# A fused gated cross-attention block: one transpose of a batch's maxima in place of two, and the maxima added to the queries in two parts

## The chip, the cores and the metric

The kernel runs on one core of a Trainium2 chip. The metric is the device time of one execution in microseconds (us); before the change the median of three runs is 1119.73 us (1119.67 to 1120.63).

## The reference, cut to what matters

The input is 128 batches of 128 tokens with 256 features, and a context of the same shape. Per batch (all fp32, 16 heads of D = 16 features):

```python
v = (ctx @ Wv + bv);  k = (ctx @ Wk + bk);  q = (layernorm(x) @ Wq + bq)     # 16 heads of 16
energy = einsum('nqhd,nkhd->nhqk', q, k);  energy = where(mask == 0, neg, energy)
attn = softmax(energy / sqrt(16), axis=-1)
x = x + tanh(g_xattn) * (einsum('nhqk,nkhd->nqhd', attn, v) @ Wo + bo)
x = x + tanh(g_ffn) * tanh(layernorm(x) @ W1 @ W2 @ W3 + b_ffn)
```

The softmax needs, for each head and query, the maximum over the keys. The change concerns how that maximum gets to the queries.

## The kernel before, in words

The 128 batches are worked in 64 pairs. Each engine has its own instruction list, written out by hand as a loop over t = 0..63, and semaphores between them; nothing is reordered at run time. A step of the loop has two halves, one batch each: half 0 handles batch 2t, half 1 batch 2t+1. The pair's projections, the output product and the feed-forward product of earlier pairs are put between the attention's pieces.

**The layout of a head.** The 128 partitions are four groups j of 32 rows. Each group holds one head in 16 of its rows; the four slots s = 2m + a (m, a = 0, 1) along the free axis hold the other heads, so 4 x 4 = 16 heads. `spread` (L720) writes q_aug and k_aug, 128 x 512 for each batch. It scales by `parity`, a 128 x 2 table with a one where the row is in half a of its group, so that slot s has its head's features in half a of each group of 32 rows and the other 16 rows are free. In k_aug one of the free rows is all ones (set through the bias, `one_row`, L858). In q_aug the same row later takes minus the query's maximum, so that one product of 32 rows gives score minus maximum.

**The chain of one batch i**, with the names of the code:

1. `scores(i)` (TensorE, L546): 32 matmuls give the scores, queries on partitions, in ps_s, four banks of PSUM; 16 small bf16 matmuls (L552) add the mask. It waits for `t_masked` of batch i-2, since ps_s is one buffer that two kinds of scores share.
2. `maxima(i)` (VectorE, L938): one reduction 128 x 2048 to 128 x 16 writes minus the maxima into neg_max, a tile of 144 columns: slot s of group j goes to column 16 + 32j + s.
3. `turn_max(i)` (TensorE, L563): two fp32 transposes by the identity, of columns 0 to 127 and of columns 16 to 143, into ps_x. The first puts the maxima of slot s into row 32j + 16 + s, the second into row 32j + s; all other rows are zero.
4. `append_max(i)` (VectorE, L944): one `tensor_tensor` 128 x 512 adds both results to q_aug, the first to the slots with a = 0, the second to those with a = 1, and signals `q_ready2`.
5. `scores_T(i)` (TensorE, L573): 32 matmuls give score minus maximum, keys on partitions, in ps_s again. It waits for `q_ready2` of batch i and for `max_ready` of batch i+1, since `maxima(i+1)` must have read ps_s.
6. `mask_transposed(i)` (VectorE, L949) adds the mask while it moves 128 x 2048 from ps_s to probs; ScalarE takes the exponents (L748); `weigh_values(i)` (TensorE, L585) multiplies by the values into ps_x and waits for `q_ready2` of batch i+2 too, since ps_x held its turned maxima.

In TensorE's list one half runs: `turn_max(i-1)`, `scores(i)`, `weigh_values(i-3)`, the output product (half 0, L455) or the turning of y and three quarters of v (half 1, L442 and L510), `scores_T(i-1)`, then the projections of q and k (half 0, L448) or the rest of v, the feed-forward product and the turning of x (half 1, L510, L455, L442).

In VectorE's list half 1 of a step, with the `append_max` that opens it, runs: `append_max`, moments of y (L964, L968), moments of x (L931), `maxima(2t+1)`, reciprocals (L974), statistics of x (L925), `low_of_y` (L905), `mask_transposed`. Half 0 runs: `append_max`, `low_of_x` (L905), statistics of x (L925), `maxima(2t)`, a transpose of the context (L910), the residual (L957), `mask_transposed`.

Of the kernel before, what the change touches and what calls it, by code (L numbers as in the profile page):

```python
# [10 lines left out]
ALU = mybir.AluOpType  # L11
AX = mybir.AxisListType

P = 128
E = 256
KT = E // P
H = 16
D = E // H
G = 4
ROWS = 2 * D  # L20
SLOTS = H // G
PAIR = 2
TOK = PAIR * P
# [7 lines left out]
def gated_xattn_block(nc, x, ctx, mask, g_xattn, g_ffn, Wv, bv, Wk, bk, Wq, bq, Wo, bo,  # L31
# [7 lines left out]
    out_v = out.rearrange("(p b) s e -> s p b e", b=PAIR)  # L39

    with ExitStack() as stack:
        def sb(name, shape, dt=F32):
            return stack.enter_context(nc.sbuf_tensor(name, shape, dt))

        def psum(name, shape):
            return stack.enter_context(nc.psum_tensor(name, shape, F32))

        def sem(name):
            return stack.enter_context(nc.semaphore(name))


        ident = sb("ident", [P, P])
# [5 lines left out]
        wq_raw, wk_raw, wv_raw, wo_raw = (sb(n, [P, KT, E]) for n in ("wq_raw", "wk_raw", "wv_raw", "wo_raw"))  # L58
# [3 lines left out]
        parity, one_row = sb("parity", [P, 2]), sb("one_row", [P, KT, 2])  # L62
# [16 lines left out]
        q_aug = [sb(f"q_aug{i}", [P, PAIR, SLOTS, P]) for i in range(2)]  # L79
        k_aug = [sb(f"k_aug{i}", [P, PAIR, SLOTS, P]) for i in range(2)]  # L80
        v_ones = [sb(f"v_ones{i}", [P, PAIR, H, 2 * D]) for i in range(V_RING)]
        neg_max = [sb(f"neg_max{i}", [P, D + P]) for i in range(2)]
        probs = [sb(f"probs{i}", [P, G, SLOTS, P]) for i in range(2)]
        a_den = [sb(f"a_den{i}", [P, 2, KT, PAIR, P]) for i in range(2)]
        a_rows, den_wide, a_norm = (sb(n, [P, KT * TOK]) for n in ("a_rows", "den_wide", "a_norm"))
# [15 lines left out]
        ps_s = psum("ps_s", [P, G, SLOTS, P])  # L101
        ps_x = psum("ps_x", [P, SLOTS, P])
# [20 lines left out]
        ffn_landed, out_landed, bf_landed = sem("ffn_landed"), sem("out_landed"), sem("bf_landed")  # L123
# [30 lines left out]
        def wait(eng, semaphore, value):  # L154
            if value > 0:
                eng.wait_ge(semaphore, value)
# [18 lines left out]
            return a.rearrange("p a b -> p (a b)")  # L175

        def heads_of(slot):
            return [(j, (slot // 2) * 2 * G + 2 * j + slot % 2) for j in range(G)]


        @block.sync
        def _(sp):
            def load_weight(dst, src, landed):
                sp.dma_start(dst[:], src.rearrange("(k p) n -> p k n", p=P)).then_inc(landed, 16)
# [4 lines left out]
            def load_x(p):  # L189
                wait(sp, y_ready, p - X_RING + 1)  # L190
                sp.dma_start(x_in[p % X_RING][:], x_v[:, p]).then_inc(x_landed[p % X_RING], 16)

            def load_ctx(p):
                wait(sp, ctx_turned, p - 1)
                if p == 0:
                    sp.dma_start(ctx_in[0][:], ctx_v[:, 0]).then_inc(ctx_landed[0], 16)
                    return
                for a in range(G):
                    rows = slice(a * 32, (a + 1) * 32)
                    sp.dma_start(ctx_in[p % 2][rows].rearrange("c n (b e) -> c (n b) e", e=64),  # L200
                                 ctx[PAIR * p:PAIR * (p + 1), :, a * 64:(a + 1) * 64].rearrange("n (b c) e -> c (n b) e", c=32)
                                 ).then_inc(ctx_landed[p % 2], 16)
# [18 lines left out]
            def wo_rows(src, m):  # L221

                return src.rearrange("(m j a d) n -> m a j d n", m=KT, a=2, d=D)[m]

            def load_later():
                for dst, src in ((w2_s, W2), (w3_s, W3), (w1_s, W1)):
                    load_weight(dst, src, ffn_landed)
                for m in range(KT):
                    for a in range(2):
                        sp.dma_start(wo_raw[a * 64:(a + 1) * 64, m, :], wo_rows(Wo, m)[a]).then_inc(out_landed, 16)  # L230
                        sp.dma_start(bv_c[a * 64:(a + 1) * 64, m:m + 1],
                                     bv.rearrange("(m j a d) -> m a j d", m=KT, a=2, d=D)[m, a].unsqueeze(2),
                                     allow_slow_non_contiguous=True).then_inc(out_landed, 16)
                sp.dma_start(bo_raw[:], bo.rearrange("(a n) -> a n", a=1)).then_inc(out_landed, 16)
                sp.dma_start(bf_wide[:], b_ffn.rearrange("(a n) -> a n", a=1).to_broadcast([P, E])).then_inc(bf_landed, 16)
                load_ctx(2)
                load_x(3)
# [33 lines left out]

            load_first()
            load_later()
            for t in range(NP):
                if is_pair(t - 7):
# [12 lines left out]
            y3, y2, y1, last = NP - 4, NP - 3, NP - 2, NP - 1  # L288
# [146 lines left out]
        def _(pe):  # L435
# [121 lines left out]
            def turn_max(i):  # L557
                pe.wait_ge(max_ready, i + 1)
                if i == 0:
                    pe.wait_ge(farT_ready, 1)  # L560
                wait(pe, a_ready, i - 2 if i < NB - 1 else i - 1)
                for a in range(2):
                    last = nc.tensor.transpose(ps_x[:, a, :], neg_max[i % 2][:, a * D:a * D + P], ident[:])  # L563
                last.then_inc(max_turned, 1)

            def scores_T(i):
                p, n = i // 2, i % 2
# [9 lines left out]
            def weigh_values(i):  # L577
                p, n = i // 2, i % 2
                pe.wait_ge(v_ready, p + 1)
                pe.wait_ge(probs_ready, i + 1)  # L580
                pe.wait_ge(q_ready2, i + 3 if i < NB - 3 else min(i + 2, NB))
                wait(pe, a_ready, i)
                for s in range(SLOTS):
                    for j, h in heads_of(s):
                        last = nc.tensor.matmul(ps_x[j * ROWS:(j + 1) * ROWS, s, :], v_ones[p % V_RING][:, n, h, :],  # L585
                                                probs[i % 2][:, j, s, :], start=True, stop=True, tile_position=(0, j * ROWS))
                last.then_inc(pv_done, 1)
# [51 lines left out]
            for t in range(NP):  # L639
                for half in range(2):  # L640
                    i = 2 * t + half
                    if is_batch(i - 1):
                        turn_max(i - 1)
# [31 lines left out]
                    product(i)  # L675
            y4, y3, y2, y1, last = (NP - n for n in range(5, 0, -1))
            turn_max(NB - 1)
            scores_T(NB - 1)
            weigh_values(NB - 2)
# [18 lines left out]
        def _(act):  # L698
# [21 lines left out]
            def spread(dst, src, scale, bias, ready):  # L720
                for m in range(KT):
                    for a in range(2):
                        last = nc.scalar.activation(dst[:, :, 2 * m + a, :], src[:, m * TOK:(m + 1) * TOK].rearrange("p (n q) -> p n q", q=P),  # L723
                                                    ACT.Identity, bias=bias[:, m, a:a + 1], scale=scale[:, a:a + 1])
                last.then_inc(ready, 1)

            def spread_k(p):
                act.wait_ge(k_done, p + 1)
                wait(act, t_done, 2 * (p - 1))
                spread(k_aug[p % 2], bank("k", p), parity, k_bias, k_ready)  # L730
# [96 lines left out]
            y4, y3, y2, y1, last = (NP - n for n in range(5, 0, -1))  # L827
# [21 lines left out]
        def _(dve):  # L849
            def setup_spreads():  # L850
                dve.wait_ge(consts_ready, IDENT)
                nc.vector.tensor_reduce(parity[:], ident[:].rearrange("p (j a d) -> p a j d", j=G, a=2), AX.XY, ALU.add)
                columns = ident[:].rearrange("p (j c) -> p c j", j=G)
                nc.vector.tensor_reduce(ident_sum[:], columns, AX.X, ALU.add)

                for m in range(KT):
                    for a in range(2):
                        last = nc.vector.tensor_reduce(one_row[:, m, a:a + 1], columns[:, 2 * m + a + D * (1 - a), :], AX.X, ALU.add)  # L858
                last.then_inc(spreads_ready, 1)

            def setup_biases():
# [72 lines left out]
            def maxima(i):  # L934
                dve.wait_ge(s_done, i + 1)
                wait(dve, max_turned, i - 1)
                out_v = neg_max[i % 2][:, D:].rearrange("p (j c) -> p j c", j=G)[:, :, 0:SLOTS]
                nc.vector.tensor_reduce(out_v, ps_s[:], AX.X, ALU.max, negate=True).then_inc(max_ready, 1)  # L938

            def append_max(i):  # L940
                dve.wait_ge(max_turned, i + 1)
                q = q_aug[i // 2 % 2][:, i % 2].rearrange("p (m a) q -> p m (a q)", a=2)
                rows = ps_x[:, 0:2, :].rearrange("p a q -> p (a q)").unsqueeze(1).to_broadcast([P, KT, 2 * P])
                nc.vector.tensor_tensor(q, q, rows, ALU.add).then_inc(q_ready2, 1)  # L944

            def mask_transposed(i):
                dve.wait_ge(t_done, i + 1)
# [99 lines left out]
            for t in range(NP):  # L1047
# [6 lines left out]
                if is_batch(2 * t):  # L1054
                    maxima(2 * t)
# [28 lines left out]
            y4, y3, y2, y1, last = (NP - n for n in range(5, 0, -1))  # L1084
# [59 lines left out]
```

## Time and profile before

| | |
|---|---|
| median of three runs | 1119.73 us (1119.67 to 1120.63) |
| span of the profiled execution | 1118.3 us, 1.4 us under that median |
| TensorE matmuls (PE) | 1073.6 us busy, 96% of the span |
| VectorE (DVE) | 966.1 us, 86% |
| ScalarE (ACT) | 826.3 us, 74% |
| GpSimd (POOL) | 774.2 us, 69% |
| granted TensorE clock, mean | 0.988 of full speed |

The span is the time from the first to the last instruction of one execution; the rest of a run's time lies around it. An engine's busy time counts its own instructions; matmuls are pipelined and their ends are modelled, so 96% says only that one matmul or another was nearly always in flight. PE is TensorE's matmuls and PEld its weight loads. L563 is line 563 of the kernel.

### The profile page before, as it was taken

The page shows a single profiled execution, that of the slowest core. Times are in us where ns is not written, and L with a number is a line of the kernel's source. Part 1 is how long each engine was busy: PE and PEld are TensorE (multiplying, and loading weights), DVE is VectorE, ACT ScalarE, POOL GpSimd, SP SyncE. Part 2 cuts the span into 40 slices and gives each one's busy share as a digit, 9 for nine tenths or more (in the row PEclk, how much of TensorE's full clock was granted, in tenths as well). Part 3 has the DMA queues.
Part 4 walks back from the last instruction along what each step waited for, and adds up shares of the span by engine and source line. Part 5 has one row for each costly group of instructions (what it writes and reads, how often), then busy time and mean ns, then how long its engine had stood idle before and what let it go on. Part 6 is the DMA issues. An engine that isn't in the chain of part 4 may idle for free.

```text
span 1118.3 us, 45477 instructions
## 1 busy us (share of the span) xinstructions
PE 1073.6 (96%) x18979; PEld 941.8 (84%) x18979; DVE 966.1 (86%) x1272; ACT 826.3 (74%) x1275; POOL 774.2 (69%) x1185
## 2 busy tenths in 40 slices
PE   5989999999999999999999999999999999999975
PEld 4777888888888888888888888888888888888865
DVE  4788888988988988898888898898889889889876
ACT  4465877877887787787777787778778778777842
POOL 5245677777777776776777777777777777777653
PEclk9899999999999999999999999999999999999997
DMA  6134344334434433433433443443443344343232
GB/s 167 30 89 117 77 120 136 102 106 134 110 114 119 128 107 107 135 108 98 136 103 104 136 108 112 123 124 106 112 135 106 102 135 108 113 121 108 71 116 77
DMA packets 160189, 124.78 MB, mean 112 GB/s; under 512 B 91889, under 2 KB 126962, under 8 KB 159986
## 3 DMA queue, kind: packets, MB, share of 16 engines
q1 hardware_dynamic: 159842, 121.61, 38.8%
q8 instruction: 152, 2.49, 1.0%
q14 instruction: 51, 0.42, 0.1%
q10 hardware_dynamic: 144, 0.26, 0.1%
HBM read 69.41 MB, written 51.38 MB: 108 GB/s over the span
## 4 chain that ended last, share of the span: by engine, by line
PE 89%; DVE 5%; issue 2%; SPq 2%; DMA 1%; ACT 0%; DVEq 0%
PE ps_m L455 17%; PE ps_m L448 16%; PE ps_s L573 13%; PE ps_s L546 12%; PE ps_x L585 11%; PE ps_m L510 8%; PE ps_m L442 5%; PE ps_s L552 4%; PE ps_x L563 2%; DVE neg_max L938 2%; DVE probs L949 2%; DMA a_rows<-scratch_a 0%; DMA den<-a_den 0%; SPq L200 0%; PE ps_m L598 0%
## 5 line engine op out<-in xcount | busy, mean ns | idle before, releaser
L949 DVE TENSOR_TENSOR probs<-ps_s,far_T 128x2048 f32<-128x2048 f32 x128 | 293.3, 2292 | 36.8 <-PE ps_s L573 36.6
L938 DVE TENSOR_REDUCE neg_max<-ps_s 128x16 f32<-128x2048 f32 x128 | 291.3, 2276 | 6.4 <-PE ps_s L552 6.3
L748 ACT ACTIVATE probs<-probs 128x2048 f32<-128x2048 f32 x128 | 244.5, 1910 | 7.9 <-DVE probs L949 7.7
L723 ACT ACTIVATE q_aug<-ps_m,q_bias,q_scale 128x256 f32<-128x256 f32 x256 | 123.7, 564 | 161.9 <-PE ps_m L448 152.4
L573 PE MATMUL ps_s<-q_aug,k_aug 32*128 32x128 f32 x4096 | 152.8, 284 | 7.4 <-DVE neg_max L938 3.3
L546 PE MATMUL ps_s<-k_aug,q_aug 32*128 32x128 f32 x4096 | 151.1, 284 | 6.4 <-DVE probs L949 6.1
L573 PEld LDWEIGHTS ps_s<-q_aug,k_aug 32*128 32x128 f32 x4096 | 129.9, 187 | 27.2 <-issue 17.4
L944 DVE TENSOR_TENSOR q_aug<-q_aug,ps_x 128x512 f32<-128x512 f32 x128 | 88.0, 687 | 74.0 <-PE ps_x L563 74.0
L546 PEld LDWEIGHTS ps_s<-k_aug,q_aug 32*128 32x128 f32 x4096 | 126.9, 187 | 28.3 <-issue 28.3
L585 PE MATMUL ps_x<-probs,v_ones 128*32 128x128 f32 x4096 | 139.2, 277 | 3.9 <-issue 2.3
L388 POOL TENSOR_TENSOR y<-y,th 128x512 f32<-128x512 f32 x58 | 74.1, 1278 | 88.7 <-ACT th L769 88.7
L585 PEld LDWEIGHTS ps_x<-probs,v_ones 128*32 128x32 f32 x4096 | 104.9, 110 | 32.9 <-issue 32.9
L723 ACT ACTIVATE k_aug<-ps_m,k_bias,parity 128x256 f32<-128x256 f32 x256 | 124.2, 583 | 0.0
L510 PE MATMUL ps_m<-wv_s,cT 128*128 128x256 f32 x756 | 123.1, 299 | 0.0
L324 POOL TENSOR_TENSOR ln_t<-stat,c_eps 128x4 f32<-128x4 f32 x69 | 14.9, 216 | 153.0 <-DVE stat L931 141.5
L455 PE MATMUL ps_m<-wo_s,aT 128*128 128x256 f32 x768 | 110.0, 293 | 2.7 <-DVE aT L905 2.5
L455 PEld LDWEIGHTS ps_m<-wo_s,aT 128*128 128x128 f32 x768 | 97.0, 192 | 15.8 <-issue 15.4
L448 PE MATMUL ps_m<-xT,wq_s 128*128 128x256 f32 x768 | 108.4, 290 | 0.7 <-DVE xT L905 0.7
L510 PEld LDWEIGHTS ps_m<-wv_s,cT 128*128 128x128 f32 x756 | 98.6, 191 | 8.9 <-issue 1.5
L448 PE MATMUL ps_m<-cT,wk_s 128*128 128x256 f32 x768 | 103.2, 284 | 2.0 <-DVE wk_s L876 2.0
L455 PE MATMUL ps_m<-wf_s,yT 128*128 128x256 f32 x756 | 102.5, 286 | 2.8 <-DVE yT L905 2.8
L448 PEld LDWEIGHTS ps_m<-xT,wq_s 128*128 128x128 f32 x768 | 95.2, 188 | 8.9 <-issue 1.8
(122 smaller groups left out, 1958.2 us busy)
## 6 DMA issues: line engine op xcount, KB each, us to landing
scratch_a<-a_den SPq DMA_DIRECT2D x64, 512.0 KB, 3.1
x_in<-in_x SPq DMA_DIRECT2D x64, 256.0 KB, 3.7
a_rows<-scratch_a SPq DMA_DIRECT2D x64, 256.0 KB
den_wide<-scratch_r SPq DMA_DIRECT2D x64, 256.0 KB
out<-y SPq DMA_DIRECT2D x64, 256.0 KB, 5.3
ctx_in<-in_ctx SPq DMA_DIRECT2D x252, 64.0 KB, 3.8
den<-a_den SPq DMA_DIRECT2D x128, 8.0 KB
scratch_r<-den_r SPq DMA_DIRECT2D x64, 16.0 KB, 1.4
```

The costliest lines, as they stand in the source:

```text
L388: nc.gpsimd.tensor_tensor(tile, tile, flat(th[:]), ALU.add).then_inc(res_ready, 1)
L448: last = nc.tensor.matmul(dst[:, m * TOK:(m + 1) * TOK], w[:, a, k, m * P:(m + 1) * P], src[:, b, k, :], start=(n == 0), stop=(n == len(TE ...
L455: last = nc.tensor.matmul(dst[:, i * E:(i + 1) * E], src[:, a, k, i * P:(i + 1) * P], w[:, b, k, :], start=(n == 0), stop=(n == len(TERMS) ...
L510: last = nc.tensor.matmul(dst[:, i * E:(i + 1) * E], cT[:, a, k, i * P:(i + 1) * P], wv_s[:, b, k, :], start=(n == 0), stop=(n == len(TERM ...
L546: nc.tensor.matmul(ps_s[:, j, s, :], q_aug[p % 2][rows, n, s, :], k_aug[p % 2][rows, n, s, :], start=(s == 0), stop=False, tile_position=( ...
L573: last = nc.tensor.matmul(ps_s[:, j, s, :], k_aug[p % 2][rows, n, s, :], q_aug[p % 2][rows, n, s, :], start=True, stop=True, tile_position ...
L585: last = nc.tensor.matmul(ps_x[j * ROWS:(j + 1) * ROWS, s, :], v_ones[p % V_RING][:, n, h, :], probs[i % 2][:, j, s, :], start=True, stop= ...
L723: last = nc.scalar.activation(dst[:, :, 2 * m + a, :], src[:, m * TOK:(m + 1) * TOK].rearrange("p (n q) -> p n q", q=P), ACT.Identity, bia ...
L748: nc.scalar.activation(tile, tile, ACT.Exp).then_inc(probs_ready, 1)
L938: nc.vector.tensor_reduce(out_v, ps_s[:], AX.X, ALU.max, negate=True).then_inc(max_ready, 1)
L944: nc.vector.tensor_tensor(q, q, rows, ALU.add).then_inc(q_ready2, 1)
L949: nc.vector.tensor_tensor(probs[i % 2][:].rearrange("p j s q -> p (j s) q"), ps_s[:].rearrange("p j s q -> p (j s) q"), far_T[:].unsqueeze ...
```

## The change

The maxima of a slot are written where the slot needs them, so that a single transpose gives all of them: slot s = 2m + b of group j goes to column 32j + 16b + m of neg_max, and after the transpose to row 32j + 16b + m. Each row half b of the one result now belongs to the slots of that b, and the other half holds the other slots' maxima, which must not be added. So VectorE adds in two parts, one for each b, each with `scalar_tensor_tensor`: the turned rows times `parity[:, b]` (one in half b, zero elsewhere) plus the query tile. The features of a slot move to the half that is free of its maxima: 1 - a for a, in `heads_of`, in the load of Wo and bv, in `spread` and in `one_row`.

```diff
-        neg_max = [sb(f"neg_max{i}", [P, D + P]) for i in range(2)]
+        neg_max = [sb(f"neg_max{i}", [P, P]) for i in range(2)]
...
-            return [(j, (slot // 2) * 2 * G + 2 * j + slot % 2) for j in range(G)]
+            return [(j, (slot // 2) * 2 * G + 2 * j + 1 - slot % 2) for j in range(G)]
...
-                        sp.dma_start(wo_raw[a * 64:(a + 1) * 64, m, :], wo_rows(Wo, m)[a]).then_inc(out_landed, 16)
+                        sp.dma_start(wo_raw[a * 64:(a + 1) * 64, m, :], wo_rows(Wo, m)[1 - a]).then_inc(out_landed, 16)
...
-                for a in range(2):
-                    last = nc.tensor.transpose(ps_x[:, a, :], neg_max[i % 2][:, a * D:a * D + P], ident[:])
-                last.then_inc(max_turned, 1)
+                nc.tensor.transpose(ps_x[:, 0, :], neg_max[i % 2][:], ident[:]).then_inc(max_turned, 1)
...
-                        last = nc.scalar.activation(dst[:, :, 2 * m + a, :], src[:, m * TOK:(m + 1) * TOK].rearrange("p (n q) -> p n q", q=P),
+                        last = nc.scalar.activation(dst[:, :, 2 * m + 1 - a, :], src[:, m * TOK:(m + 1) * TOK].rearrange("p (n q) -> p n q", q=P),
...
-                        last = nc.vector.tensor_reduce(one_row[:, m, a:a + 1], columns[:, 2 * m + a + D * (1 - a), :], AX.X, ALU.add)
+                        last = nc.vector.tensor_reduce(one_row[:, m, a:a + 1], columns[:, m + D * (1 - a), :], AX.X, ALU.add)
...
-                out_v = neg_max[i % 2][:, D:].rearrange("p (j c) -> p j c", j=G)[:, :, 0:SLOTS]
-                nc.vector.tensor_reduce(out_v, ps_s[:], AX.X, ALU.max, negate=True).then_inc(max_ready, 1)
+                out_v = neg_max[i % 2][:].rearrange("p (j b c) -> p j c b", j=G, b=2)[:, :, 0:KT, :]
+                nc.vector.tensor_reduce(out_v, ps_s[:].rearrange("p j (m b) k -> p j m b k", b=2), AX.X, ALU.max, negate=True).then_inc(max_ready, 1)
...
-                q = q_aug[i // 2 % 2][:, i % 2].rearrange("p (m a) q -> p m (a q)", a=2)
-                rows = ps_x[:, 0:2, :].rearrange("p a q -> p (a q)").unsqueeze(1).to_broadcast([P, KT, 2 * P])
-                nc.vector.tensor_tensor(q, q, rows, ALU.add).then_inc(q_ready2, 1)
+                rows = ps_x[:, 0, :].unsqueeze(1).to_broadcast([P, KT, P])
+                for b in range(2):
+                    q = q_aug[i // 2 % 2][:, i % 2].rearrange("p (m b) q -> p b m q", b=2)[:, b]
+                    last = nc.vector.scalar_tensor_tensor(q, rows, parity[:, b:b + 1], q, ALU.mult, ALU.add)
+                last.then_inc(q_ready2, 1)
```

## Rows read from the trace of the kernel before

**Rows 1.** The page: busy time by engine, and the chain's shares by engine.
```profile
PE 1073.6 (96%) x18979; PEld 941.8 (84%) x18979; DVE 966.1 (86%) x1272; ACT 826.3 (74%) x1275; POOL 774.2 (69%) x1185
...
PE 89%; DVE 5%; issue 2%; SPq 2%; DMA 1%; ACT 0%; DVEq 0%
```

**Rows 2.** The chain in order of time: start us, us, piece; 480 to 530 us.
```profile
498.92 0.22 PE ps_x L563 x2
...
507.39 0.22 PE ps_x L563 x2
...
515.31 0.22 PE ps_x L563 x2
```

**Rows 3.** Groups by line, shapes apart: busy us, mean ns, idle before them.
```profile
L949 DVE TENSOR_TENSOR probs<-ps_s,far_T 128x2048 f32<-128x2048 f32 x128 | 293.3, 2292 | 36.8 <-PE ps_s L573 36.6
...
L944 DVE TENSOR_TENSOR q_aug<-q_aug,ps_x 128x512 f32<-128x512 f32 x128 | 88.0, 687 | 74.0 <-PE ps_x L563 74.0
...
L563 PE MATMUL ps_x<-ident,neg_max 128*128 128x128 f32 x256 | 49.1, 274 | 4.1 <-DVE neg_max L938 4.1
```

**Rows 4.** Timeline of PE, 506.9 to 520.9 us: start us, us, instruction.
```profile
507.23 0.38 PE L563 MATMUL ps_x<-ident,neg_max 128*128 128x128 f32 x2
...
511.74 1.17 PE L573 MATMUL ps_s<-q_aug,k_aug 32*128 32x128 f32 x32
...
515.15 0.38 PE L563 MATMUL ps_x<-ident,neg_max 128*128 128x128 f32 x2
515.46 1.17 PE L546 MATMUL ps_s<-k_aug,q_aug 32*128 32x128 f32 x32
516.57 0.43 PE L552 MATMUL ps_s<-far,ident 32*32 32x512 bf16 x16
516.93 1.08 PE L585 MATMUL ps_x<-probs,v_ones 128*32 128x128 f32 x32
...
519.56 1.04 PE L573 MATMUL ps_s<-q_aug,k_aug 32*128 32x128 f32 x25
```

**Rows 5.** Timeline of DVE over the same stretch; in brackets the idle time before.
```profile
507.65 0.69 DVE L944 TENSOR_TENSOR q_aug<-q_aug,ps_x 128x512 f32<-128x512 f32 x1 [0.95 <-PE ps_x L563]
...
509.33 2.26 DVE L938 TENSOR_REDUCE neg_max<-ps_s 128x16 f32<-128x2048 f32 x1
...
512.97 2.29 DVE L949 TENSOR_TENSOR probs<-ps_s,far_T 128x2048 f32<-128x2048 f32 x1 [0.19 <-PE ps_s L573]
515.57 0.69 DVE L944 TENSOR_TENSOR q_aug<-q_aug,ps_x 128x512 f32<-128x512 f32 x1 [0.31 <-PE ps_x L563]
516.17 0.68 DVE L905 TENSOR_TENSOR xT<-ps_m,xT 128x512 fp32r<-128x512 f32 x1
516.77 0.42 DVE L925 BATCH_NORM_STATS2 stat<-x_in 128x6 f32<-128x256 f32 x1
517.11 2.29 DVE L938 TENSOR_REDUCE neg_max<-ps_s 128x16 f32<-128x2048 f32 x1
```

**Rows 6.** Timeline of DVE, 476.4 to 479.3 us.
```profile
476.54 2.26 DVE L938 TENSOR_REDUCE neg_max<-ps_s 128x16 f32<-128x2048 f32 x1
```

**Rows 7.** Timeline of PE, 476.4 to 479.3 us.
```profile
478.95 0.61 PE L573 MATMUL ps_s<-q_aug,k_aug 32*128 32x128 f32 x12 [0.29 <-DVE neg_max L938]
```

**Rows 8.** Timeline of DVE, 63.9 to 65 us.
```profile
64.19 0.48 DVE L901 TENSOR_SCALAR bo_wide<-ps_m,tgates 128x256 f32<-128x256 f32 x1 [0.99 <-PE ps_m L625]
64.59 0.68 DVE L944 TENSOR_TENSOR q_aug<-q_aug,ps_x 128x512 f32<-128x512 f32 x1
```

**Rows 9.** Timeline of DVE, 1084.5 to 1086.5 us.
```profile
1085.24 0.75 DVE L997 SCALAR_TENSOR_TENSOR y<-th,tgates,y 128x512 f32<-128x512 f32 x1
1085.90 0.68 DVE L905 TENSOR_TENSOR yT<-ps_m,yT 128x512 fp32r<-128x512 f32 x1
```

**Rows 10.** Groups by line, shapes apart: two short reductions of the setup.
```profile
L854 DVE TENSOR_REDUCE ident_sum<-ident 128x32 f32<-128x128 f32 x1 | 0.4, 358 | 0.0
...
L852 DVE TENSOR_REDUCE parity<-ident 128x2 f32<-128x128 f32 x1 | 0.3, 286 | 0.7 <-POOL ident L316 0.7
```

More of the change, by code:

```diff
@@ L229, in load_later @@
                     for a in range(2):
-                        sp.dma_start(wo_raw[a * 64:(a + 1) * 64, m, :], wo_rows(Wo, m)[a]).then_inc(out_landed, 16)
+                        sp.dma_start(wo_raw[a * 64:(a + 1) * 64, m, :], wo_rows(Wo, m)[1 - a]).then_inc(out_landed, 16)
                         sp.dma_start(bv_c[a * 64:(a + 1) * 64, m:m + 1],
-                                     bv.rearrange("(m j a d) -> m a j d", m=KT, a=2, d=D)[m, a].unsqueeze(2),
+                                     bv.rearrange("(m j a d) -> m a j d", m=KT, a=2, d=D)[m, 1 - a].unsqueeze(2),
                                      allow_slow_non_contiguous=True).then_inc(out_landed, 16)
```

## The prediction

> **What bounds the kernel now.** I read the page's busy times and chain first. TensorE is busy 96% of the span, VectorE 86%, and the chain that ended last is 89% PE, 5% DVE [rows 1]. Taken alone that says: TensorE is the bound, VectorE has 14% to spare, and taking work from TensorE at VectorE's cost must pay. The chain, however, goes back along TensorE's own list wherever the gap is too short to look like a wait, so I read the two engines' timelines side by side over one pair of batches.
>
> The pair has two halves. In the chain L563 (the turned maxima) comes at 498.92, 507.39 and 515.31 us: 8.47 us for half 0, 7.92 for half 1, 16.39 for a pair, and 64 pairs are 1049 of the 1118 us [rows 2].
>
> Half 1 first. L563 starts at 507.23 and L573, the transposed scores, at 511.74 [rows 4]. Between these VectorE runs from L944 at 507.65, which had been idle for 0.95 us until L563 was done, through the moments to the reduction L938 at 509.33, which ends at 509.33 + 2.26 = 511.59 [rows 5]. L573 has to wait for that reduction (same buffer) and starts 0.15 us later. Is 0.15 us slack, or just the time in which the signal gets across? At 476 us there is a copy of the same place in which VectorE is a little late and the profile does call it a wait: the reduction ends at 476.54 + 2.26 = 478.80 and L573 starts at 478.95, after 0.29 us of idle [rows 6, 7]. The distance is again 0.15 us. So 0.15 us is the crossing, and in half 1 it is VectorE that releases L573: there is no slack in the stretch L563, L944, moments, L938, L573.
>
> Half 0: L563 at 515.15, L944 at 515.57, L905, L925, L938 ends at 517.11 + 2.29 = 519.40, L573 at 519.56 [rows 4, 5]. The distance is 0.16 us, so VectorE has 0.01 us to spare here. For the rest of both halves (from L573 to the next L563) TensorE works through its projections and is the bound; VectorE waits for it, 0.95 us before L944 in half 1 and 0.31 us in half 0 [rows 5].
>
> The path that sets the end therefore goes over VectorE from L563 to L573 and over TensorE from L573 to L563, twice a pair. What counts is the length of the first stretch, not an engine's total.
>
> **The change, part by part.**
>
> One transpose less. In the chain two take 0.22 us, so one takes 0.11 [rows 2]. With one, L563 ends 0.11 us earlier and L944 can start 0.11 us earlier, for it waits for exactly that in both halves. TensorE's list also gets 0.11 us shorter, but up to L573 this is no gain, since L573 waits for VectorE. Minus 0.11 us for each of the 128 batches on the VectorE stretch.
>
> The addition in two parts. Successive VectorE instructions overlap at their ends (L944 starts at 515.57, takes 0.69, and L905 starts at 516.17), so what counts is start to start: L944 costs 0.60 us now [rows 5]. The new instruction is 128 x 256, reads PSUM, and has a scalar for each partition. The trace has two near relatives. L901 has the same width, reads PSUM and has such a scalar; it takes 0.48 and its successor starts after 64.59 - 64.19 = 0.40 us [rows 8]. L997 is the same operation at twice the width: successor after 1085.90 - 1085.24 = 0.66 us [rows 9]. The price of a column comes from L949 and L944, the same operation with 2048 and 512 columns: (2292 - 687) / 1536 = 1.045 ns [rows 3], so 256 columns fewer are 0.27 us fewer and L997 becomes 0.39. I take 0.395 each, 0.79 for the two. That is 0.79 - 0.60 = +0.19 us per batch. The bound below is that the scalar costs nothing: L944 itself at half the width, 0.60 - 0.27 = 0.33 each, +0.07 us. The bound above is that the second part, which reads the same PSUM rows, doesn't overlap the first: 0.48 + 0.40 = 0.88, +0.28 us. I stay with +0.19 because two different rows give it.
>
> A rule of the Trainium skill speaks to the lower bound. The Vector Engine (DVE) Microarchitecture Reference, section "5.2 Measured stream behaviour on trn2", gives one- and two-source operations 1.0417 ns a column plus about 75 ns an instruction once they overlap. L944's step agrees (0.60 us for 512 columns), while L901's and L997's steps are some 0.06 us longer than that. By the page an instruction of 256 columns would be 0.34 us, estimated, and the addition would grow by only 0.08 us.
>
> The reduction's new output order (L938): the same 2048 elements in the same order, 16 results to other columns. I take 0. In the setup a reduction of 128 elements took 358 ns with a scattered reading order and 32 results, 286 ns without [rows 10], so 0.07 us is the bound above; I see no source of a gain.
>
> At no cost on the path: swapping halves in `heads_of`, `spread`, `one_row` and in the loads of Wo and bv keeps every count, width and queue order; no DMA is added or passed. neg_max is smaller by 16 columns, which only its setup memset sees. `q_ready2` is signalled by the second part. Two waits hang on it: L573, later and bound by L938 anyway, and L585, whose PSUM rows the addition reads. L944 ends at 516.26 now and L585 starts at 516.93, 0.67 us later [rows 4, 5]; the stretch between shrinks by 0.19 to 0.48 us, still more than the crossing of 0.15. If that cover were gone, each 0.1 us would delay L585.
>
> **The sum.** Half 1: L563 to L573 changes by 0.19 - 0.11 = +0.08 us. Half 0: +0.08 less the 0.01 to spare = +0.07. The other stretches keep their length: TensorE has the same work from L573 on, and the mask L949 starts at L573's end as now [rows 5]. After the mask, L546 at 515.46 follows the mask's end (512.97 + 2.29 = 515.26) by 0.20 us, 0.05 more than the crossing, so of the 0.11 us that its transpose gives back only 0.05 can be used. It doesn't matter, because the reduction behind it starts 0.11 us after L552's end (516.57 + 0.43) and in the changed kernel would be held by VectorE's own list. So +0.15 us a pair, x 64 = +9.6 us. I count the first and last pairs like the others; the addition stands on their path in the same way. The profiled span goes from 1118.3 to 1127.9; with the 1.4 us by which the median of the runs lies over this span, 1129.3 us. In general: with x for the growth of the addition, a pair changes by 2x - 0.23, and the break-even is at x = 0.115 us.
>
> **The rivals.**
>
> (a) The scalar is free, as by the page's 75 ns: x = 0.07, 2x - 0.23 = -0.09 us a pair, -5.8 us, 1113.9 us. For it: L944's own step. Against it: L901 and L997, the two rows with a scalar, are both longer.
>
> (b) TensorE is the bound after all, and the 0.15 us distances are chance. Then all transposes count, 128 x 0.11 = -14.1 us: 1105.6 us, VectorE's extra going into its idle time. For it: 96% busy, and nearly all 74.0 us of idle before L944 are a wait for TensorE [rows 1, 3]. Against it: the same 0.15 us in a place where the profile names VectorE [rows 6, 7]. It would need slack of at least 0.08 us in each half.
>
> (c) The added work is dearer: the two parts don't overlap (x = 0.28: +0.33 a pair, +21 us, 1140.9), or the reduction pays its 0.07 us (+0.15 + 0.14 = +0.29 a pair, +18.6 us, 1138.3); together some 1150. Against it: VectorE instructions overlap wherever they follow one another in these rows. The Trainium skill (VectorE: DVE Perf Modes, section "Two Vector instructions with no wait between them") has an instruction held only if a start quadrant changes; all tiles here start at partition 0. No row shows such a hold.
>
> (d) x happens to be near 0.115, and gain and loss cancel: within 0.2% of before, 1117.5 to 1122. That the change does not do what it says is no real case: one matmul less per batch is in the list.
>
> **How the numbers follow.** The forecast (slower by about 0.9%) 74%, (a) 8%, (b) 4%, (c) 10%, (d) 4%. The forecast's own range, x from 0.165 to 0.22, is 1126 to 1133. What a measurement can tell from no change is about 0.2%, 2.2 us. The range for 8 in 10 takes in the forecast, the cheaper half of (c) and a little on the other side for x down to 0.13 (+0.03 a pair, 1122): 1122 to 1140. Faster 0.12, same 0.05, slower 0.83.
>
> **What would show it.** In the changed trace: L573 starts 0.15 us behind the end of L938 in both halves; L563 to L573 in half 1 grows from 4.51 us, counted from the first matmul, by 0.08; from L944's start to its successor's 0.79 instead of 0.60; L573 to the next L563 as before; the pair 16.54 us instead of 16.39. The DVE busy time rises by more than PE's falls. The prediction is wrong in its mechanism if L573 starts well over 0.15 us after L938's end, and wrong in its size if the step of the new instructions isn't 0.39 to 0.40.

## The result: 1128.8 us, 0.8% slower

The changed kernel takes 1128.82 us (median of 6, 1124.98 to 1132.83) against 1119.70 for the kernel before (median of 6, 1117.75 to 1123.27). The ratio is 1.0079, 95% interval 1.0056 to 1.0102. Forecast were 1129.3 us and slower.

The profiled execution after the change, the longest of the six (1132.83 us), has a span of 1130.7 us. Its page answers to [rows 1]; busy time and instructions by engine, then the chain's shares:

```profile
PE 1071.1 (95%) x18851; PEld 934.7 (83%) x18851; DVE 985.7 (87%) x1400; ACT 827.3 (73%) x1275; POOL 772.2 (68%) x1185
...
PE 69%; DVE 23%; issue 5%; SPq 2%; DMA 1%; ACT 0%; DVEq 0%
```

TensorE has 128 matmuls fewer and is busy for 2.5 us less, VectorE has 128 instructions more and is busy for 19.6 us more. By busy share the kernel still looks bound by TensorE, 95% to 87%. But the chain, which gave VectorE 5% before, now gives it 23%: the gap before the transposed scores has become wide enough to be called a wait.

The new addition, grouped by line (busy us, mean ns, idle before), answers to L944 in [rows 3]:

```profile
L943 DVE SCALAR_TENSOR_TENSOR q_aug<-ps_x,parity,q_aug 128x256 f32<-128x256 f32 x256 | 112.1, 480 | 63.5 <-PE ps_x L562 63.5
```

Timelines of one pair, first PE and then DVE, answer to [rows 4, 5]. After the change L562 is the transpose, L571 the transposed scores, L936 the reduction, L943 the addition:

```profile
511.07 0.27 PE L562 MATMUL ps_x<-ident,neg_max 128*128 128x128 f32 x1
...
515.66 1.17 PE L571 MATMUL ps_s<-q_aug,k_aug 32*128 32x128 f32 x32 [0.18 <-DVE neg_max L936]
...
519.08 0.27 PE L562 MATMUL ps_x<-ident,neg_max 128*128 128x128 f32 x1
...
523.53 1.17 PE L571 MATMUL ps_s<-q_aug,k_aug 32*128 32x128 f32 x32
```

```profile
511.38 0.88 DVE L943 SCALAR_TENSOR_TENSOR q_aug<-ps_x,parity,q_aug 128x256 f32<-128x256 f32 x2 [0.84 <-PE ps_x L562]
512.18 0.74 DVE L964 BATCH_NORM_STATS2 stat<-y 128x6 f32<-128x256 f32 x2
...
513.25 2.26 DVE L936 TENSOR_REDUCE neg_max<-ps_s 128x16 f32<-128x2048 f32 x1
...
519.39 0.88 DVE L943 SCALAR_TENSOR_TENSOR q_aug<-ps_x,parity,q_aug 128x256 f32<-128x256 f32 x2 [0.21 <-PE ps_x L562]
520.18 0.68 DVE L903 TENSOR_TENSOR xT<-ps_m,xT 128x512 fp32r<-128x512 f32 x1
...
521.11 2.27 DVE L936 TENSOR_REDUCE neg_max<-ps_s 128x16 f32<-128x2048 f32 x1
```

Half 1: the reduction ends at 513.25 + 2.26 = 515.51 and L571 starts at 515.66, 0.15 us later. Half 0: 521.11 + 2.27 = 523.38 and 523.53, again 0.15. VectorE releases L571 in both halves now. From the transpose to L571 are 4.59 us (half 1) and 4.45 (half 0), where before the first of the two transposes was 4.51 and 4.41 ahead. The addition's step is 520.18 - 519.39 = 0.79 us in place of 0.60.

For the comparisons that follow I use the length of a pair in each trace: the time from one transpose of the maxima to the next, the median over the 55 halves of each kind between batches 14 and 123, both kinds added. It leaves out the run's ends and single stops. Before it is 8.472 + 7.922 = 16.394 us, after 8.510 + 8.005 = 16.515: +0.121 us a pair, or 7.7 us for 64 pairs, inside what the ratio's interval allows (6.3 to 11.4 us). Between these batches the granted TensorE clock is 1.00 of full speed in both traces, but for 3.4 us after the change (see "Why the prediction was right"), so the longer pair is not a matter of the clock.

### The profile page after: what moved, and what is told of

Read it like the earlier page. It is cut to its first block, busy times and chain, and to the rows that moved or that the text cites. A ratio compares the mean times of both kernels' runs of the same rounds, so it can differ in the third digit from the quotient of the medians.

```text
span 1130.7 us, 45349 instructions
## 1 busy us (share of the span) xinstructions
PE 1071.1 (95%) x18851; PEld 934.7 (83%) x18851; DVE 985.7 (87%) x1400; ACT 827.3 (73%) x1275; POOL 772.2 (68%) x1185
## 4 chain that ended last, share of the span: by engine, by line
PE 69%; DVE 23%; issue 5%; SPq 2%; DMA 1%; ACT 0%; DVEq 0%
PE ps_m L455 17%; PE ps_m L448 16%; PE ps_s L571 13%; DVE neg_max L936 13%; PE ps_s L546 7%; PE ps_x L583 6%; DVE stat L964 3%; PE ps_m L510 3%; DVE q_aug L943 3%; PE ps_m L442 2%; PE ps_s L552 2%; DVE probs L949 2%; PE ps_x L562 1%; DVE stat L968 1%; DVE stat L929 1%
## 5 line engine op out<-in xcount | busy, mean ns | idle before, releaser
L949 DVE TENSOR_TENSOR probs<-ps_s,far_T 128x2048 f32<-128x2048 f32 x128 | 293.3, 2291 | 40.2 <-PE ps_s L571 40.0
L936 DVE TENSOR_REDUCE neg_max<-ps_s 128x16 f32<-128x2048 f32 x128 | 290.3, 2268 | 5.1 <-PE ps_s L552 4.6
L571 PE MATMUL ps_s<-q_aug,k_aug 32*128 32x128 f32 x4096 | 152.8, 283 | 20.2 <-DVE neg_max L936 12.8
L943 DVE SCALAR_TENSOR_TENSOR q_aug<-ps_x,parity,q_aug 128x256 f32<-128x256 f32 x256 | 112.1, 480 | 63.5 <-PE ps_x L562 63.5
L571 PEld LDWEIGHTS ps_s<-q_aug,k_aug 32*128 32x128 f32 x4096 | 131.3, 187 | 42.9 <-issue 40.0
L546 PE MATMUL ps_s<-k_aug,q_aug 32*128 32x128 f32 x4096 | 152.0, 285 | 6.7 <-DVE probs L949 6.7
L546 PEld LDWEIGHTS ps_s<-k_aug,q_aug 32*128 32x128 f32 x4096 | 129.3, 188 | 29.3 <-issue 29.3
```

Source lines behind the costliest of these rows:

```text
L546: nc.tensor.matmul(ps_s[:, j, s, :], q_aug[p % 2][rows, n, s, :], k_aug[p % 2][rows, n, s, :], start=(s == 0), stop=False, tile_position=( ...
L571: last = nc.tensor.matmul(ps_s[:, j, s, :], k_aug[p % 2][rows, n, s, :], q_aug[p % 2][rows, n, s, :], start=True, stop=True, tile_position ...
L936: nc.vector.tensor_reduce(out_v, ps_s[:].rearrange("p j (m b) k -> p j m b k", b=2), AX.X, ALU.max, negate=True).then_inc(max_ready, 1)
L943: last = nc.vector.scalar_tensor_tensor(q, rows, parity[:, b:b + 1], q, ALU.mult, ALU.add)
L949: nc.vector.tensor_tensor(probs[i % 2][:].rearrange("p j s q -> p (j s) q"), ps_s[:].rearrange("p j s q -> p (j s) q"), far_T[:].unsqueeze ...
```

## The experiments

All ran with the kernel before beside them; its median was 1119.40 to 1121.55 us in the four sessions (1119.70 beside the changed kernel, 1121.55 beside the next four rows, 1120.99 beside the two with the new order, 1119.40 beside the last). As these differ, a comparison of medians from two sessions is good to some 2 us. The last column compares with the kernel that was edited.

| run | edited kernel | median us (runs) | ratio to before, interval | pair us | pair's change |
|---|---|---|---|---|---|
| changed kernel | before | 1128.82 (6) | 1.0079, 1.0056 to 1.0102 | 16.515 | +0.121 |
| matmuls behind the signal | changed | 1139.62 (4) | 1.0176, 1.0136 to 1.0216 | 16.639 | +0.124 |
| transpose ahead of the signal | changed | 1143.19 (4) | 1.0200, 1.0167 to 1.0234 | 16.745 | +0.230 |
| matmuls behind the signal | before | 1145.02 (4) | 1.0216, 1.0183 to 1.0249 | 16.787 | +0.393 |
| addition split only | before | 1127.41 (10) | 1.0051, 1.0025 to 1.0076 | 16.490 | +0.096 |
| new order | changed | 1101.25 (6) | 0.9832, 0.9798 to 0.9866 | 16.166 | -0.349 |
| new order | before | 1110.75 (6) | 0.9905, 0.9884 to 0.9927 | 16.340 | -0.054 |
| half 1's move only | changed | 1113.53 (5) | 0.9934, 0.9904 to 0.9963 | 16.266 | -0.249 |

**More TensorE work, behind the signal and ahead of it.** In the changed kernel, one of the edits each:

```diff
# matmuls behind the signal: in scores(i)
-                for s in range(SLOTS):
+                for s in (0, *range(SLOTS)):
# transpose ahead of the signal: in turn_max(i)
+                nc.tensor.transpose(ps_x[:, 1, :], neg_max[i % 2][:], ident[:])
                 nc.tensor.transpose(ps_x[:, 0, :], neg_max[i % 2][:], ident[:]).then_inc(max_turned, 1)
```

> The changed kernel, and in scores() the first four of the 32 matmuls are issued twice (L546, the same values written again): 4 x 0.034 = 0.14 us more TensorE work in each batch, placed behind the signal of the turned maxima, so that it does not delay VectorE's addition. Theory (VectorE's stretch from L562 to L571 is the bound, TensorE has slack there): after the change L571 starts 0.455 us behind the previous matmul in half 1 and 0.32 in half 0, where 0.21 is what an unhindered start takes; slack 0.245 and 0.11 us. So +0.00 in half 1 and +0.03 in half 0, pair 16.54 instead of 16.51, about +2 us on the changed kernel's 1128.8. Rival (TensorE's total work is the bound): +0.28 us a pair, +18 us, about 1146.

> The changed kernel, with a second transpose of the same tile issued ahead of the one that signals (into rows of ps_x that nobody reads): 0.11 us of TensorE work ahead of the signal, which VectorE's addition waits for. Theory: the stretch L562 to L571 grows by 0.11 us in each half, pair 16.51 + 0.22 = 16.73 us, +14 us, about 1143. Rival (VectorE's total work is the bound and TensorE has room): nothing, 1129. Together with the run with matmuls behind the signal: the same kind of work costs its full time ahead of the signal and next to nothing behind it.

The first expectation had the size of its own load wrong. Each of the four matmuls in the code is two instructions in the trace, so eight were added, not four; L546 takes 1.40 us instead of 1.17, +0.23 a batch. The theory's reckoning with 0.22 to 0.23 is: half 1, slack 0.245, nothing; half 0, slack 0.11, +0.11 to 0.12. Measured: half 1 from 8.005 to 8.009, half 0 from 8.510 to 8.630. Rows of half 1, PE and then DVE:

```profile
515.57 0.27 PE L562 MATMUL ps_x<-ident,neg_max 128*128 128x128 f32 x1
515.77 1.40 PE L546 MATMUL ps_s<-k_aug,q_aug 32*128 32x128 f32 x40
...
520.15 1.17 PE L571 MATMUL ps_s<-q_aug,k_aug 32*128 32x128 f32 x32
```

```profile
517.74 2.26 DVE L936 TENSOR_REDUCE neg_max<-ps_s 128x16 f32<-128x2048 f32 x1
```

TensorE has 0.23 us more to do between L562 and L571, yet the distance is 4.58 us as without it, and L571 still comes 0.15 us behind the reduction's end at 520.00. The transpose ahead of the signal is only 0.11 us of work, half as much, and costs all of it in both halves, 0.230 a pair. Per microsecond of added TensorE work the pair pays 0.124 / 0.46 = 0.27 behind the signal and 0.230 / 0.22 = 1.0 ahead of it. The median of the first run is 1139.62 us where 1131 were expected, 10.8 above the changed kernel's. Of these 0.124 x 64 = 7.9 are the pair's; what the rest is was not found. Its profiled execution, 4.7 us longer than the median, has more stops of TensorE than the other traces, see the end. The second run has 1143.19 us, as expected. Neither the full +0.46 a pair (TensorE's total as the bound) nor zero for the transpose (VectorE's total as the bound) was found.

**The same matmuls in the kernel before** (the first edit above).

> The kernel before, and in scores() the first four matmuls issued twice: 0.14 us more TensorE work per batch behind the signal of the turned maxima. Theory: before the change the slack of TensorE's list up to L573 is 0.06 us in half 1 and none in half 0, so +0.08 and +0.14, pair 16.39 + 0.22 = 16.61 us, +14 us, about 1134. Rival (VectorE alone is the bound already before the change): nothing, 1120.

With 0.23 instead of 0.14 the theory has +0.17 in half 1 and +0.23 in half 0; measured 8.090 - 7.922 = +0.168 and 8.697 - 8.472 = +0.225. With the load at its true size the pairs give 25 us, and the median is 23.5 above the kernel before in its session. So before the change TensorE's list was already the limit in half 0 and 0.06 us short of it in half 1. The same load costs 0.393 us a pair here and 0.124 there: the change has moved the bound to VectorE.

**The split alone**, in the kernel before, with both transposes:

```diff
-                nc.vector.tensor_tensor(q, q, rows, ALU.add).then_inc(q_ready2, 1)
+                for b in range(2):
+                    q = q_aug[i // 2 % 2][:, i % 2].rearrange("p (m b) q -> p b m q", b=2)[:, b]
+                    last = nc.vector.tensor_tensor(q, ps_x[:, b, :].unsqueeze(1).to_broadcast([P, KT, P]), q, ALU.add)
+                last.then_inc(q_ready2, 1)
```

> The kernel before with one edit: both transposes stay, and the addition is done by two tensor_tensor of 128x256 without a scalar, one for each parity of the slots. Theory: each starts 0.60 - 0.27 = 0.33 us before its successor, together 0.67 instead of 0.60, +0.07 us in half 1 and +0.06 in half 0, pair 16.39 + 0.13 = 16.52 us, +8 us, about 1128. Then the scalar is some 0.12 us of the changed kernel's growth of 0.19. Rival (VectorE's addition is hidden in its idle time of 0.95 and 0.31 us before L944): no change, 1119.7.

VectorE in half 0 of this kernel:

```profile
517.80 0.76 DVE L944 TENSOR_TENSOR q_aug<-ps_x,q_aug 128x256 f32<-128x256 f32 x2 [0.32 <-PE ps_x L563]
518.47 0.68 DVE L905 TENSOR_TENSOR xT<-ps_m,xT 128x512 fp32r<-128x512 f32 x1
```

The step is 0.67 us, +0.07, and the pair grows by 0.096: 0.069 in half 1 and 0.027 in half 0. Half 1 is as worked out; in half 0 some 0.03 us are missing, of which the reduction, shorter there (2.27 instead of 2.29 us, though its output order is the old one), accounts for 0.02. The idle time before L944, 0.32 us here, hides nothing. Of the changed kernel's growth of 0.19 the split is 0.07, and 0.12 come from going over from `tensor_tensor` to `scalar_tensor_tensor` with a scalar per partition, 0.06 for each instruction. No run separates the scalar from the other operation; L901 in [rows 8], with such a scalar and a single multiplication, has the same 0.06 more.

**VectorE's list in another order.** If the bound is the stretch and not VectorE's total, work can leave the stretch and go where VectorE is idle:

```diff
-                if is_pair(t + 3):
-                    stats_of_x(t + 3, 0)
                 if is_batch(2 * t):
                     maxima(2 * t)
...
+                if is_pair(t - 4):
+                    moments_of_y(t - 4)
                 if is_batch(2 * t):
                     append_max(2 * t)
-                if is_pair(t - 4):
-                    moments_of_y(t - 4)
                 if t > 0 and is_pair(t + 2):
                     moments_of_x(t + 2)
+                if is_pair(t + 3):
+                    stats_of_x(t + 3, 0)
```

> The changed kernel with VectorE's list in another order, nothing added or left out: the moments of y (L964, L968; 0.78 us) run ahead of the addition that opens half 1, in VectorE's idle time of 0.84 us there, instead of behind it; the statistics of x of half 0 (0.33 us) move from half 0's stretch between addition and reduction to half 1's. Theory (the stretch L562 to L571 is the bound by 0.245 us in half 1 and 0.11 us in half 0): VectorE is covered in both halves, TensorE becomes the bound, L571 starts 0.21 us behind the previous matmul; the pair falls from 16.51 to about 16.18 us (one transpose less than the kernel before: 16.39 - 0.22), -21 us on 1128.8, about 1108, faster than both kernels. Rival (VectorE's total busy time is the bound, 87% of the span and 15.2 us of each pair with its crossings): the order changes nothing, 1129.

> The same new order of VectorE's list in the kernel before. Theory: there VectorE's stretch exceeded TensorE's own by only 0.06 us in half 1 and not at all in half 0, so the pair falls from 16.39 to about 16.33 us, -4 us, about 1116; the difference to the changed kernel with the same order is then the one transpose per batch, 0.15 to 0.22 us a pair, 10 to 14 us. Rival (the order is what counts and the transpose nothing): both kernels with the new order take the same time.

The changed kernel in this order takes 1101.25 us, 2.4% less than without it (1101.25 / 1128.82), and is faster than both kernels. The pair is 16.166 us, as expected (16.18), which is 22 us of the 28; the median is 7 us below the expected 1108 for another reason: batch 13's transpose comes at 131.65 us in this trace instead of 137.64, 6 us that the theory did not have. Its PE and DVE over one half 1 and the beginning of half 0:

```profile
512.45 0.27 PE L562 MATMUL ps_x<-ident,neg_max 128*128 128x128 f32 x1
...
516.77 1.17 PE L571 MATMUL ps_s<-q_aug,k_aug 32*128 32x128 f32 x32
...
520.20 0.27 PE L562 MATMUL ps_x<-ident,neg_max 128*128 128x128 f32 x1
520.46 1.17 PE L546 MATMUL ps_s<-k_aug,q_aug 32*128 32x128 f32 x32
```

```profile
511.83 0.74 DVE L964 BATCH_NORM_STATS2 stat<-y 128x6 f32<-128x256 f32 x2
...
512.77 0.86 DVE L943 SCALAR_TENSOR_TENSOR q_aug<-ps_x,parity,q_aug 128x256 f32<-128x256 f32 x2
...
514.30 2.29 DVE L936 TENSOR_REDUCE neg_max<-ps_s 128x16 f32<-128x2048 f32 x1 [0.20 <-PE ps_s L552]
...
518.02 2.29 DVE L949 TENSOR_TENSOR probs<-ps_s,far_T 128x2048 f32<-128x2048 f32 x1
```

The idle time before the addition, 0.84 us, is gone, filled by the moments of y. In its place the reduction now waits for TensorE (0.20 us, for L552). It ends at 516.59, L571 comes 0.18 us later, more than the crossing: TensorE's own list is the limit, 4.32 us from L562 instead of 4.59. VectorE's busy time is 998.1 us, more than in any kernel above and 90% of the span, in the fastest of them; as a total it never was the bound. What is left over VectorE is the mask: L949 ends at 518.02 + 2.29 = 520.31 and L546 follows at 520.46, just the crossing of 0.15.

The order alone gives the kernel before 0.054 us a pair, 3.5 us in all, as its 0.06 us of slack said. Its median is 10.2 us below the kernel before in the same session (1110.75 against 1120.99), not the 4 that were expected; the rest lies at the run's start, where batch 13's transpose comes at 129.7 us instead of 137.6. With the order in both, the single transpose is worth 16.340 - 16.166 = 0.174 us a pair, 11 us; the medians are 9.5 apart. In half 1 that is all of the transpose, 0.11, in half 0 only 0.06, for there L546 then waits for the mask: the prediction's "of the 0.11 us that its transpose gives back only 0.05 can be used". So the change's saving was real and only hidden.

**One of the two moves.** In the changed kernel, the moments of y alone are moved:

> The changed kernel with one of the two moves alone: the moments of y run ahead of the addition that opens half 1, the statistics of x stay between addition and reduction in half 0. Theory (each half has its own bound, and its excess over TensorE's list adds): half 1 falls by its excess of 0.245 us, from 8.005 to 7.76, half 0 stays VectorE's and at 8.51; pair 16.27 us instead of 16.515, -16 us on 1128.8, about 1113, between the changed kernel and the one with both moves (1101). Rival (the two halves share their slack, so that time won in one is lost in the other): no better than 1129, or as good as both moves.

Half 1 falls from 8.005 to 7.761, half 0 stays at 8.505: pair 16.266 us, median 1113.53. Batch 13's transpose comes at 137.0 us here, so the earlier start above belongs to the other move, that of the statistics of x; why was not looked into. In the timeline of half 0 of this kernel the reduction's end (301.72 + 2.27 = 303.99) still is 0.15 us ahead of L571 (304.14).

Each half has its own bound, and they add.

## Why the prediction was right, step by step

The place of the bound was right: L563 to L573 over VectorE, the rest over TensorE. More exactly, before the change TensorE's own list was the limit of that stretch in half 0, by the 0.01 us that the prediction took off as "to spare", and in half 1 it was 0.06 us short of being it; that the path goes over VectorE in both halves holds only after the change. It came from reading one constant distance, 0.15 us, in two timelines, where the chain of waits named TensorE throughout. The runs with the load ahead of and behind the signal show it without that argument.

The addition was sized right: 0.79 us predicted from L901 and L997, 0.79 measured (480 ns each, the steps overlapping). Rival (a), the free scalar, is out: the split without scalars has 0.67 and the addition with them 0.79. The Trainium skill's 75 ns per instruction (Vector Engine (DVE) Microarchitecture Reference, section "5.2 Measured stream behaviour on trn2") holds for the two without scalars, 0.67 / 2 - 0.267 = 0.07 us (0.267 is 256 columns at the 1.045 ns worked out from [rows 3]), and falls short by 0.06 us for each with one.

The transpose: 0.11 us, as the run with one more ahead of the signal confirms (0.230 for two). Rival (b), TensorE as the bound, would have had 1105.6 us. It is out by the measured time and by the two loads that were added. The saving it counts on, 0.22 us a pair, comes only with the cover that the new order gives, and there for the most part (0.174). Rival (c): the parts overlap, and the reduction takes no longer in its new output order. Rival (d), no change within 0.2%, lies below the interval of the ratio, which begins at 0.56%.

Where the size was off. The pair grew by 0.121 and not 0.15. Half 1 is +0.083 against +0.08. Half 0 is +0.038 against +0.07. In it the stretch grew by 0.047 and not 0.07, for the reduction takes 2.27 us there now, 0.02 less; and from L571 to the next transpose 0.01 was won. The term that was mis-sized is the reduction's: "I take 0", bounded only from above ("I see no source of a gain"), where half 0 has -0.02. It is not the new output order that shortens it, for the split alone, with the old order, has the same 2.27.

The sum took 64 equal pairs. The trace gives 0.121 for the steady ones, 6.7 us over the 55 pairs between batches 14 and 123. Batch 13's transpose starts at 137.64 us in both traces; but batch 0's starts at 26.06 us instead of 27.09, so the first pairs paid about 1.0 us too, hidden in these two traces by a setup that was shorter by as much (over all nine traces batch 0's transpose starts between 23.4 and 27.1). The profiled execution is 12.4 us longer than before. Beside the 6.7 us these are 2.0 us between batches 14 and 123 and 3.7 us behind batch 123, and both go with the clock. The 2.0 come from one place: behind a stop of TensorE at 642 us the granted clock is 0.50, the lower of its two levels, for 3.4 us, and the half that it falls into is 3.1 us longer than the median; at the same place of TensorE's list the new order and half 1's move alone stop too, keep a clock of 1.00 and lose 1.0 and 1.1 us. The stretch behind batch 123 takes 74.9 us at a mean granted clock of 0.89 before and 78.6 at 0.83 after; the changed kernel with more matmuls has 74.9 at 0.95 there, half 1's move alone 78.8 at 0.83. So it differs between traces of the same code at the run's end, and mostly along with the clock; which is cause and which effect there is not shown. The median's +9.1 us is 7.7 of the pairs and 1.4 that the steady state does not explain, and that it lies so near the forecast of +9.6 is partly luck.

## What to carry to other kernels

Before work moves from a busy engine to one with spare time, find the stretch in which the busy one waits for the other's result: a start that keeps the same short distance to the other's end, while its distance to its own predecessor varies, is a release, whatever share the page gives. Price the new instructions from start to start, and expect a split to pay the fixed part twice and the scalar on top. When such a change loses, look for idle time of the helper ahead of the stretch: moving unrelated work there turned +0.8% into -1.7%, of which 6 us, some 0.5%, came from an earlier start of the loop that nobody had foreseen. Look at the run's two ends apart from its steady pairs, and at the granted clock there, before a median is taken as the price of a change.

## What the runs showed of the hardware

An fp32 `scalar_tensor_tensor` with a scalar per partition costs 0.06 us more on VectorE than a `tensor_tensor` of the same size (0.396 against 0.336 us from start to start, 128x256 with one source in PSUM). That L901, with one scalar and one operation, is as much dearer speaks for the scalar as the cause; a run with a constant in its place was not made.

The same reduction of 128x2048 from PSUM takes 2.29 us when it starts 0.11 us behind the last matmul into that buffer, which is as soon as it is released, and 2.26 to 2.28 when VectorE comes to it later, 0.17 us or more behind that matmul. Half 0 before the change [rows 5] is of the first kind, half 0 after it (0.25 us behind) and half 0 of the split alone (0.17) of the second, and in the new order both halves take 2.29 throughout. Among the later ones the distance does not order the times: 2.26 at 0.21 us in half 1 of the changed kernel with more matmuls, 2.28 at 0.29 us in half 0 of the one with the added transpose. Whether the distance is the cause was not tested.

TensorE stops now and then in the midst of a group of matmuls for 0.3 to 1.7 us, with no wait that the profile shows. The stops are not strewn at random: kernels with the same list of TensorE instructions stop at the same instruction of it. These are the kernel before and then the one with the addition split, both in the transposed scores of batch 59 with 7 of the 32 matmuls to go:

```profile
521.79 0.50 PE L573 MATMUL ps_s<-q_aug,k_aug 32*128 32x128 f32 x7 [1.18 <-issue]
```

```profile
523.50 0.50 PE L573 MATMUL ps_s<-q_aug,k_aug 32*128 32x128 f32 x7 [0.67 <-issue]
```

The kernel before in the new order stops there too (0.36 us). The changed kernel, its new order and half 1's move alone, which share another list, all stop in L571 of batch 67 with 3 matmuls to go (0.40, 0.66 and 0.67 us) and in that of batch 73 with 13 to go (1.15, 0.56 and 0.62 us). Not every such place stops in every run, and the length varies. Their number differs from list to list: the changed kernel with more matmuls has 8.0 us of gaps over 0.25 us between 200 and 1050 us, where the changed kernel has 2.4; and the kernel before with the same matmuls added has 0.4. What TensorE waits for there stays open.

In three of the nine traces the granted clock falls to 0.50 for 3.4 us in the steady part, each time about 1 us behind the end of such a stop (of 1.15, 1.74 and 1.22 us). The half with the stop is then 3.1 to 3.5 us longer than the median, the stop included. Other stops of 1.1 to 1.5 us had no fall behind them.
